# Attention with 16-bit halves: every fourth low part of the probabilities moved from POOL to DVE

## What is computed

```python
scores = jnp.einsum('bgrqd,bgkd->bgrqk', q, k) / jnp.sqrt(jnp.float32(HD))
scores = jnp.where(causal_mask[None, None, None, :, :], -jnp.inf, scores)
scores = jnp.where(padding_mask[:, None, None, None, :], -jnp.inf, scores)
w = jax.nn.softmax(scores, axis=-1)
out = jnp.einsum('bgrqk,bgkd->bgrqd', w, v)
...
x = x + jnp.tanh(g_xattn[0]) * _L0_xattn_ref(_layernorm(x, axis=-1), ctx_2048, ...)
```

## Time and profile before

| what | value |
|---|---|
| runs of the kernel | 1722.57, 1726.62, 1729.61 us (median 1726.62) |
| span of the profiled execution (its own time as shown) | 1722.0 us |
| PE busy over the span | 1587.8 us (92%) |
| DVE, ACT, POOL busy | 973.1, 709.2, 824.3 us |
| first and last low part (L1109) | 78.0 and 502.8 us |

### The profile page before, as it was taken

One profiled execution on the slowest core, in us unless ns is written; L12 is line 12 of the kernel. 1 busy time (PEld: TensorE's weight loads), 2 busy tenths in 40 slices (PEclk: granted clock), 3 DMA queues, 4 the chain that ended last, 5 costly groups with the idle time before them and its releaser, 6 DMA issues. The chain is left out here.

```text
span 1722.0 us, 29300 instructions
## 1 busy us (share of the span) xinstructions
PE 1587.8 (92%) x10826; PEld 829.3 (48%) x10826; DVE 973.1 (57%) x1947; ACT 709.2 (41%) x1311; POOL 824.3 (48%) x853
## 2 busy tenths in 40 slices
PE   5769999999877999899999989999999999999998
PEld 3336665665443444345656544444444444444443
DVE  5736666778736999845665543377454333211146
ACT  3268888888855655532232321211111111222221
POOL 3478887877853545443452434344333532112134
PEclk9989999999878999999999999999999999999999
DMA  6745444322333555444554426447454754477746
GB/s 182 160 102 112 99 106 109 93 67 72 92 73 84 110 119 114 93 86 86 96 120 95 78 74 156 110 105 153 92 101 101 154 101 95 109 173 172 168 138 195
DMA packets 453955, 195.68 MB, mean 114 GB/s; under 512 B 395500, under 2 KB 418286, under 8 KB 453816
## 3 DMA queue, kind: packets, MB, share of 16 engines
q1 hardware_dynamic: 448136, 175.19, 46.0%
q0 software_dynamic: 5680, 18.62, 4.1%
HBM read 77.17 MB, written 22.81 MB: 58 GB/s over the span
## 5 line engine op out<-in xcount | busy, mean ns | idle before, releaser
L1109 POOL TENSOR_TENSOR a_pl<-a_prob,a_ph 128x512 f16<-128x512 f32 x256 | 295.2, 1166 | 72.7 <-ACT a_prob L996 72.3
L1199 DVE TENSOR_REDUCE a_mx<-bank 128x2 f32<-128x512 f32 x256 | 173.3, 686 | 97.1 <-PE bank L690 95.5
L140 PE MATMUL bank<-XTh,d_whs 128*128 128x512 f16 x512 | 194.9, 381 | 4.2 <-PEq L89 2.4
L141 PE MATMUL bank<-XTl,d_whs 128*128 128x512 f16 x512 | 194.7, 380 | 0.0
L142 PE MATMUL bank<-XTh,d_wls 128*128 128x512 f16 x512 | 194.6, 380 | 0.0
L995 ACT ACTIVATE a_ph<-bank 128x512 f16<-128x512 f32 x256 | 153.9, 601 | 73.3 <-PE bank L710 35.9
L2384 POOL CAST d_cut<-d_raw 128x512 f16<-128x512 f32 x90 | 56.2, 624 | 227.7 <-DMA d_raw<-in_L_ffn_sw 146.8
L996 ACT ACTIVATE a_prob<-bank 128x512 f32<-128x512 f32 x256 | 154.4, 603 | 0.0
L2304 DVE TENSOR_TENSOR d_hid<-d_hid,bank 128x512 f32<-128x512 f32 x64 | 43.9, 686 | 172.1 <-PE bank L142 168.2
L2295 ACT ACTIVATE d_hid<-bank 128x512 f32<-128x512 f32 x64 | 38.2, 597 | 204.7 <-PE bank L142 204.7
L2299 ACT ACTIVATE d_hh<-d_hid 128x512 f16<-128x512 f32 x64 | 40.3, 630 | 194.7 <-DVE d_hid L2304 194.7
(11 more groups left out here) (349 smaller groups left out, 3996.4 us busy)
## 6 DMA issues: line engine op xcount, KB each, us to landing
d_raw<-in_L_ffn_w SPq DMA_DIRECT2D x48, 256.0 KB, 3.1
d_raw<-in_L_ffn_sw SPq DMA_DIRECT2D x42, 256.0 KB, 3.1
made<-e_y SPq DMA_DIRECT2D x39, 256.0 KB
a_stage<-in_L_ffn_w_fc SPq DMA_DIRECT2D x32, 256.0 KB, 2.9
a_stage<-in_L_ffn_w_proj SPq DMA_DIRECT2D x32, 256.0 KB, 3.1
a_fbuf<-in_ctx SPq DMA_DIRECT2D x16, 256.0 KB, 3.5
rows<-f_cut SPq DMA_DIRECT2D x16, 256.0 KB, 2.5
out_x<-X SPq DMA_DIRECT2D x16, 256.0 KB, 2.4
```

Of the source, the lines that this page charges most:

```text
L140: nc.tensor.matmul(out_ap, lhi, rhi, start=first, stop=False)
L141: nc.tensor.matmul(out_ap, lhi, rlo, start=False, stop=False)
L1109: nc.gpsimd.tensor_tensor(pl[:, n % NP, :], prob[:, n % 2, :], ph[:, n % NP, :], ALU.subtract).then_inc(ev["L"], 1)
L1199: nc.vector.tensor_reduce(mx[:, h, tt, half, 2 * (g % 4):2 * (g % 4) + 2], bank[BS + m % 2][:, :].rearrange("p (r k) -> p r k", r=2), AX_X ...
```

## The change

The steps with n % 4 == 2 lose their instruction on POOL. DVE gets it, as the first instruction of the next step (n % 4 == 3), ahead of `normalise`, `magnitude` and the maxima of that step. It counts in an event of its own, `LD`; PE and ACT wait for `LD` or `L`, whichever belongs to the step in question. These are 8 of 32 steps in each block, 64 of 256 in all.

```diff
-             "nt", "nc", "ng0", "ng1", "ST", "E", "L", "AV", "ON", "To0", ...
+             "nt", "nc", "ng0", "ng1", "ST", "E", "L", "LD", "AV", "ON", "To0", ...
...
+    def low_wait(eng, b, n):
+
+        if n < 0:
+            b, n = b - 1, n + NS
+        if b < 0:
+            return
+        if n % 4 == 2:
+            eng.wait_ge(ev["LD"], b * NS // 4 + n // 4 + 1)
+        else:
+            eng.wait_ge(ev["L"], b * (NS - NS // 4) + n + 1 - (n + 1) // 4)
...
-                wait("L", b, n + 3, NS)
+                low_wait(pe, b, n)
...
-                    wait("L", b, n + 1, NS)
+                    low_wait(act, b, n - 2)
...
-            pool.sem_inc(ev["L"], 2)
...
-                    pool.wait_ge(ev["E"], b * NS + n + 3)
-                    nc.gpsimd.tensor_tensor(pl[:, n % NP, :], prob[:, n % 2, :], ph[:, n % NP, :],
-                                            ALU.subtract).then_inc(ev["L"], 1)
+                    if n % 4 != 2:
+                        pool.wait_ge(ev["E"], b * NS + n + 3)
+                        nc.gpsimd.tensor_tensor(pl[:, n % NP, :], prob[:, n % 2, :], ph[:, n % NP, :],
+                                                ALU.subtract).then_inc(ev["L"], 1)
...
                 for n in range(NS):
+                    if n % 4 == 3:
+                        m = n - 1
+                        wait("E", b, m + 3, NS)
+                        nc.vector.tensor_tensor(pl[:, m % NP, :], prob[:, m % 2, :], ph[:, m % NP, :],
+                                                ALU.subtract).then_inc(ev["LD"], 1)
```

More of the change, by code:

```diff
@@ L383, in phase_a @@
              "lk0", "lk1", "hv0", "hv1", "lv0", "lv1", "tq", "tq0", "tq1", "tk", "cq", "ck", "S", "M", "nm",
-             "nt", "nc", "ng0", "ng1", "ST", "E", "L", "AV", "ON", "To0", "To1", "hO0", "hO1", "lO0", "lO1", "O0", "O1", "x0", "x1", "ch")
+             "nt", "nc", "ng0", "ng1", "ST", "E", "L", "LD", "AV", "ON", "To0", "To1", "hO0", "hO1", "lO0", "lO1", "O0", "O1", "x0", "x1", "ch")
     ev = {n: sem("a_" + n) for n in names}
```

## The result

The changed kernel takes 1735.39 us in the median of 5 runs (1731.15 to 1740.23), the kernel before 1726.62. The ratio over the paired runs is 1.0059, 95% interval 1.0038 to 1.0079, so the change costs 6.6 to 13.6 us; 1736.8 was forecast. The profiled execution of the changed kernel is its slowest, 1740.23 us with a span of 1738.5, so the profiles lie 16.5 us apart where the medians lie 8.8.

What follows compares the result with a forecast made beforehand. PE was taken to set the pace in blocks 1 to 5 and ACT in the last. Terms 2.6 + 0.8 + 2.2 + 5.6 - 1.0 = +10.2 us on 1726.6 gave 1736.8 us, own range 1731 to 1743, 8-in-10 range 1720 to 1746.

Steps and rivals of the forecast that it cites:

- Block 7, +5.6: Last block: low part delays `magnitude`, then `sign` and exponentials; 6.4 us at steps 3, 11, 15, 27, less 0.8.
- The relief of 0.8: Block 7, steps 22 and 23: POOL gets ahead with its cast and low half, -0.8 us.
- Blocks 1 to 4, steps 3 to 6, +2.6: DVE's low part makes the maxima of step 4 late and PE waits: 0.5 in block 1, 0.7 each in 2 to 4.
- I take 0.7 for each of the three: Blocks 2, 3 and 4: PE's added wait in step 6 for the maxima of step 4, 0.7 us each.
- Step 27, +0.8: Blocks 0 to 3: PE's wait at step 28 for the low half of k and v grows 0.2 us each.
- Blocks 4 and 6, weight pieces, +2.2: `magnitude` late behind the low part: PE's step 14 in block 4 1.2 late; block 6 0.65 and 0.35.
- Block 0, -1.0: After ACT's long wait, three moved low parts let POOL catch up: 1.4 us gained, less 0.4 for late maxima.
- the maxima of the other steps have a step of slack: Blocks 1 to 4: maxima other than step 4's cost nothing; without slack each would cost up to 0.6 us.
- The operation: The low part on DVE: 0.69 us median, up to 1.66 while POOL is busy, mean near 1.0; 1.16 on POOL.
- relief: Rival: each moved low part 0.47 us shorter where POOL or ACT sets the pace, 9.4 us faster, 1717.2 us; chance 0.18.
- It comes to nothing: Rival: block 7's delays fall into PE's gaps or the port is freer; +3.5 us, 1730 us; chance 0.27.
- worse: Rival: delays also in blocks 5 and 6, 4 to 5 us, and block 7's clock lower, 3.4; 1745 us; chance 0.13.

Runs made afterwards that it cites:

- magnitude first: The changed kernel with DVE's weight-piece scaling ahead of the low part where both fall into one step: 1729.29 us, ratio 1.0029 to the kernel before.
- left out: The changed kernel with the low parts of steps 2, 6, ... 30 made by nobody, PE multiplying by zeros: 1718.86 us, ratio 0.9966 to the kernel before.
- the four profiles named above: Four follow-up kernels with no low part moved in block 6 ahead of this place, nor at its turn; block 6 took 52.0 to 52.1 us.
- the versions: Follow-up kernels moving other sets of low parts to DVE, or dropping them; for block 0, those that move or drop steps 10 and 14.
- the control: Also called none moved: the kernel before, POOL making every low part, with only the weight piece's scaling at the head of its DVE step: 1725.79 us, ratio 1.0002.
- Not 30: The changed kernel with the weight piece's scaling ahead of the low part, and step 30's low part kept on POOL: 1727.07 us, ratio 1.0026 to the kernel before.
- block 7 only: Every fourth step's low part on DVE in block 7 alone, blocks 0 to 6 as in the kernel before: 1731.78 us, ratio 1.0042.

## Why the prediction was right, and where it wasn't

The time was 1.4 us under the forecast, and by the ratio (+10.2 us) the sum of +10.2 was met. The largest term and its mechanism were right. That the sum fits so closely is luck: two terms were too large, one was missing, and their errors cancelled. From the profile, by the step at which each jump comes:

- **Block 7, +5.6: right.** Measured +6.0, and +6.2 from magnitude first. The chain was low part, `magnitude`, `sign`, exponentials, as forecast at steps 3, 11, 15 and 27, each 1.7 us later than before (1.1 at 27), where 1.75, 1.8, 1.7 and 1.15 were forecast. Steps 19 and 23 were costed at nothing, and they cost nothing, for ACT's wait for PE went down from 3.1 us to 1.8. Step 25 came in addition: `sign` waited 1.0 us for a transfer, which put the exponentials behind it some 0.5 us back. The relief of 0.8 isn't seen apart.
- **Blocks 1 to 4, steps 3 to 6, +2.6: the size too large, the mechanism right in blocks 1 and 3 alone.** Measured by the end of step 7: +0.2, +0.4, +0.3, +0.1, in all +1.0. PE's waits in blocks 2, 3 and 4 went from 0.69, 0.81 and 0.81 to 1.12, 1.30 and 1.00, where "about 1.5" was forecast. The term that was mis-sized is "I take 0.7 for each of the three". In block 3 all that stands behind the low part began 1.06 us later, not 1.3 to 1.4, and `a_ve` gave back 0.78 of it. In blocks 1 and 3 left out has no wait for these maxima and the changed kernel one of 1.3, so there the low part makes it. In blocks 2 and 4 left out waits 1.12 and 1.29 without any low part on DVE: there POOL's `ctx_low`, brought forward by the relief, holds `a_ve`, and the +0.4 of block 2 isn't shown to be DVE's.
- **Step 27, +0.8:** +0.1 in each of the four blocks. Twice too large.
- **Blocks 4 and 6, weight pieces, +2.2: right in block 4, by luck in block 6.** Block 4 jumped 1.1 us at step 13, 1.2 was forecast, and magnitude first took it away. In block 6 1.0 was forecast; `sign` waited 1.47 at step 6, the steps 4 to 8 took 1.5 us more, and step 23 took nothing. But of the 1.45 us by which `magnitude` came later than the turn of the block made it, 0.60 is the low part (0.65 was forecast) and 0.78 is the small L1261 that met POOL's low part (0.93 us instead of 0.15). That meeting alone costs 1.2 to 1.3 us in the four profiles named above, with nothing moved there, so the 1.5 isn't shown to be the change's.
- **Block 0, -1.0:** -1.3 between the starts of steps 11 and 16 in the changed kernel, -0.6 to -1.2 in the versions, 0 to -0.4 with nothing moved there. Right. The block as a whole, -0.8, says little, since the control has -1.1.
- **Not in the sum:** the turn of a block. The low part of step 30 stands ahead of the last maxima and of what follows them: +1.3 at block 6's steps 2 and 3, and +0.9 at block 3's last step, where the sum of the weights' magnitudes waits for DVE. With 0.3 in block 1, which the versions don't repeat, it makes +2.5, which "the maxima of the other steps have a step of slack" had excluded. Not 30 removed the first two.
- **The operation:** 0.69 in the median as read from the later phase, but a mean of 0.79, not 1.0, since most find POOL idle. One line of the kernel after:

```profile
L1337 DVE TENSOR_TENSOR a_pl<-a_prob,a_ph x64: 674/692/1548, 83.3 to 516.2; 128x512 f16<-128x512 f32 x64
```

Of the rivals, relief was real in part: 5.9 us when it is free, but DVE pays 16 for it. "It comes to nothing" fell with block 7 (and its 3.5 us doesn't follow from its terms: 2.8 and 0.3 for each of the blocks 1 to 5 make 4.3). Of "worse" the blocks 5 and 6 were 0.3 and 2.9 longer, and block 7's clock stayed as it was (0.79 against 0.78).

The steps and the clock's share account for the pair of profiles: 1.0 + 0.4 + 2.5 + 1.1 + 1.5 + 0.3 (block 5) + 6.0 - 0.8 = 12.0, and 1.1 for block 4's first steps, where the clock was lower: 13.1, against 12.8 between the two profiles' blocks (440.3 and 427.5 us). The ratio over all runs gives 10.2, so some of these steps are scatter of a single profile; block 6's is the likeliest.

## What to carry to other kernels

When work goes to an engine that has time to spare, ask not how long the instruction is but what stands behind its wait in the engine's list: here 64 instructions of 0.7 us cost some 16 us of delays, and moving one independent instruction ahead of the wait took some 5 of them back (ratios 1.0059 and 1.0029). Price the places apart: the same move costs nothing in steps with slack, and all of it at a step without, and the turn from one iteration to the next is such a place. A time that seems to come from a block should be checked against a control with nothing moved, since single stretches here scattered by more than the effects. Such a jump often has a cause that the trace shows: look for a small instruction that takes several times as long as in another profile.

## What the runs showed of the hardware

The stretch of the long instructions went both ways, but seldom. Of the 64 low parts on DVE, 12 took 0.84 to 1.55 us; each began while POOL was in an instruction of 1.15 us or more, and ended 0.55 us after it. Of POOL's 192, 5 took more than 1.25 (1.64 at most), and in all POOL lost about 1.3 us that way. The prediction's question, whether a moved instruction gives POOL back 0.47 us or the full 1.16, was thus decided for the full 1.16, not because the two don't exclude each other (the lengths agree with a wait for the whole instruction, as the Trainium skill has it, "SBUF — State Buffer", section "Who interferes with whom") but because both wait for the same exponentials, and in most steps POOL has nothing to do while DVE makes the low part. DVE's small instructions can profit (`a_ve` of block 3 went from 1.16 to 0.38 us) or lose (`a_ve` of block 2 went from 0.75 to 1.18 in left out). The maxima, which read PSUM, stayed at 0.67 to 0.69 us in all 256.

TensorE's clock goes with much of the scatter. Windows of 66 to 79.5 us, ahead of the change's first instruction, of the kernel before and of the kernel after:

```profile
66.00:79.50 13.50, 10.02 (x77) 5.03 (x78) 11.49 (x21) 4.53 (x10) 5.03 (x7) 1.00 0.25 54
```

```profile
66.00:79.50 13.50, 9.65 (x54) 4.67 (x55) 10.14 (x18) 2.53 (x5) 4.03 (x5) 0.78 0.27 59
```

The granted clock is 1.00 in one and 0.78 in the other (a mix of 2.4 and 1.2 GHz), though both kernels have the same instructions up to there; the kernel after is later and so has fewer of them in the window. Over the same instructions it lost about 1 us more. The same happened in block 4's first 5 us (1.00 before, 0.66 in block 7 only) and made about 1 us in most of the profiles. Over the 12 runs of magnitude first the mean clock went from 0.966 (1736.11 us) to 0.977 (1726.31 us), so a thousandth of it goes with some 0.9 us. Single blocks scatter for other reasons too: block 6 by the meeting of two instructions shown above, and block 0 at step 18, where POOL's cast waited 2.04 us for a transfer in the kernel before and 0.94 in none moved.
